# Three graph layers: from dense count and attention strips to sums over edge lists fetched by row

## What is computed

```python
# first layer: GCN with self loops, residual and layer norm
h = x @ W0;  norm = dinv[row] * dinv[col]
x1 = layernorm(x + segment_sum(h[row] * norm, col) + b0)
# then rgat_conv twice: 4 heads of 192 (then ELU), and 1 head of 768
xr = einsum('nd,rdf->rnf', x, W)
oi, oj = xr[etype, dst], xr[etype, src]
alpha = leaky_relu(oi @ q + oj @ k, 0.2)
e = exp(alpha - segment_max(alpha, dst)[dst])
out = segment_sum(e / segment_sum(e, dst)[dst] * oj, dst) + b
# result: layernorm(x1 + out2)
```

## Time and profile before

| | us |
|---|---|
| median of three runs | 1782.49 (1778.65 to 1787.3) |
| the profiled execution | 1783.22 |
| its span, first to last instruction | 1781.4 |
| mean granted TensorE clock | 0.941 of full |

### The profile page before, as it was taken

How to read it: one execution, slowest core, us unless ns; L and a number is a source line. 1 busy time by engine, 2 the same in 40 slices (tenths; PEclk the granted TensorE clock), 3 DMA queues, 4 the chain that set the end, 5 groups by cost and what they waited for, 6 DMA issues and landing times. The chain is left out here.

```text
span 1781.4 us, 27924 instructions
## 1 busy us (share of the span) xinstructions
PE 1589.1 (89%) x10121; PEld 1403.0 (79%) x10121; DVE 1240.1 (70%) x1980; ACT 580.8 (33%) x876; POOL 98.2 (6%) x58
## 2 busy tenths in 40 slices
PE   4999788978878799799979997959999989999996
PEld 4675354545548799799979997957999989999996
DVE  7346766656418999998999899943664275656774
ACT  2332122323312443354335434423222232224522
POOL 1000000000013001300310040000000000000000
PEclk8999899999988899999989998978999999999998
DMA  8674043245466655566366654426776646645652
GB/s 210 230 244 146 10 95 80 81 90 114 87 187 178 194 177 195 178 207 229 97 195 189 208 174 143 130 79 198 221 236 212 229 163 212 212 169 197 209 205 79
DMA packets 175693, 297.80 MB, mean 167 GB/s; under 512 B 35787, under 2 KB 118093, under 8 KB 175061
## 3 DMA queue, kind: packets, MB, share of 16 engines
q1 hardware_dynamic: 175476, 296.04, 54.3%
q10 hardware_dynamic: 96, 0.12, 0.0%
HBM read 227.41 MB, written 68.70 MB: 166 GB/s over the span
## 5 line engine op out<-in xcount | busy, mean ns | idle before, releaser
L1091 PE MATMUL ah_ps<-ah_xr,ah_T 125*125 125x194 f32 x2400 | 406.4, 333 | 41.2 <-issue 37.8
L1091 PEld LDWEIGHTS ah_ps<-ah_xr,ah_T 125*125 125x125 f32 x2400 | 403.0, 191 | 43.6 <-issue 38.6
L1666 PE MATMUL sl_ps<-sl_masks,sl_wH 125*125 125x256 f32 x1800 | 322.8, 282 | 10.6 <-DVE sl_wL L1506 9.6
L1666 PEld LDWEIGHTS sl_ps<-sl_masks,sl_wH 125*125 125x125 f32 x1800 | 275.6, 187 | 12.6 <-DVE sl_wL L1506 6.4
L923 ACT ACTIVATE ah_T<-ah_T,ah_kq 125x625 f32<-125x625 f32 x240 | 195.9, 817 | 223.6 <-DVE ah_T L1021 223.6
L1666 PE MATMUL sl_ps<-sl_masks,sl_wL 125*125 125x256 f32 x900 | 253.7, 282 | 0.0
L1004 DVE CUSTOM_DVE_ANT_0 ah_dump<-ah_krow,ah_gap 125x1250 bf16<-125x1250 f32 x120 | 206.1, 1781 | 14.5 <-DMA ah_krow<-ah_d_k 14.4
L1021 DVE SCALAR_TENSOR_TENSOR ah_T<-ah_rows,ah_k_rest 125x625 f32<-125x625 f32 x240 | 211.0, 881 | 0.4
L1028 DVE SCALAR_TENSOR_TENSOR ah_T<-ah_T,ah_cnt 125x625 f32<-125x625 f32 x240 | 192.4, 802 | 19.1 <-DMA ah_cnt<-d_C 17.4
L1666 PEld LDWEIGHTS sl_ps<-sl_masks,sl_wL 125*125 125x125 f32 x900 | 168.5, 187 | 0.0
L612 PE MATMUL fr_ps<-fr_col_hot,fr_row_hot 125*128 x516 | 119.0, 364 | 42.7 <-DVE fr_col_hot L406 38.1
(11 more groups left out here) (189 smaller groups left out, 2057.5 us busy)
## 6 DMA issues: line engine op xcount, KB each, us to landing
sl_masks<-sl_d_xr SPq DMA_DIRECT2D x60, 768.0 KB, 4.3
ah_gap<-d_gap SPq DMA_DIRECT2D x120, 312.5 KB, 3.6
ah_cnt<-d_C SPq DMA_DIRECT2D x240, 156.2 KB, 3.8
sl_d_xr<-sl_xs SPq DMA_DIRECT2D x60, 384.0 KB, 4.1
ah_rows<-ah_d_rows SPq DMA_DIRECT2D x24, 625.0 KB, 5.2
fr_raw<-in_w SPq DMA_DIRECT2D x36, 384.0 KB, 5.9
d_gap<-fr_gap SPq DMA_DIRECT2D x30, 312.5 KB, 2.5
d_C<-fr_C SPq DMA_DIRECT2D x15, 625.0 KB, 10.7
```

The lines of the kernel that those rows point to most:

```text
L1091: mm = pe.matmul(o, T[:, g % TR, t * P:(t + 1) * P], xr[:, r, j], start=(first and t % 2 == 0), stop=final, skip_group_check=True)
L1666: mm = pe.matmul(flat[:, u * TW:(u + 1) * TW], a[:, i % AR, ts], xr[:, i % LR, x, fs], start=(first and u % 2 == 0 and q == 0), stop=(last ...
```

## The change

Nearly the whole program is rewritten. The dense counts `d_C` and the strips go; all three layers sum over an edge list.

- `front` sorts nothing, but gives every edge a place so that each target tile starts at a pair of chunks: 88 pairs (NPAIR), 176 chunks (NCH) of 128 places, 22528 places for 20000 edges. A running count per tile (`tensor_tensor_scan`) and two small products give the places; 160 products of one-hots (`list_part`) write the lists `edge_src`, `edge_row`, `slot_dst`, `rel_hot`, `pair_tile`. Four chunks are a quad (44 of them), eight a piece (22).
- The gap table is filled with 1e30 by 30 stores and then marked by 160 scatters of 125 two-byte zeros (`mark`), each of which waits until the one before it has landed.
- In each layer `pair` multiplies one-hots of the targets (fp32) with 128 gathered source rows (fp32, 3 KB each), two chunks accumulating in PSUM, and `add_pair` adds the result to the tile's accumulator in SBUF at an index that is read at run time. The rows come from HBM by 176 indirect DMAs a layer from GpSimd's queue, in a ring of four quads that lies over xH and xL.
- `attention_heads` and `second_layer` become one function `relation_layer`, called with 4 heads (names `fl_`) and with 1 (`sl_`). Projections are 60 units of 384 columns in both and are sent to HBM as fp32 rows with a 1 and the source term k behind each head's columns. `pick` fetches every edge's target terms by products with one-hots; `alpha`, an exponential and `weighted_hot` put each edge's weight into its one-hot. The masked maximum stays. With 4 heads its gathers start after the last unit, and so do the picks; with 1 head the maxima and picks run beside the units. x and h stay in SBUF in split form between the stages.
- In the last layer products use fp32 instead of three float32r ones.

The core of the diff:

```diff
+            def mark(c):
+                if c:
+                    pool.wait_ge(gap_marked, 16 * c)
+                pool.indirect_dma_start(cells, bass.IndirectOffsetOnAxis(ap=gap_at[:, c:c + 1], axis=0), edge_gap[:], None)\
+                    .then_inc(gap_marked, 16)
+
+            for c in range(MARKS):
+                mark(c)
+            pool.wait_ge(h0_out, 32 * NT)
+            pool.wait_ge(rows_made, 1)
+            for i in range(2):
+                pool.wait_ge(s_out[i], 32 * UNITS // 2)
+            m = MARKS
+            for c in range(NCH):
+                if c >= 4 * QR and c % 2 == 0:
+                    pool.wait_ge(pair_done, (c - 4 * QR) // 2 + 1)
+                pool.indirect_dma_start(rows(c // 4)[:, c % 4], None, d_h0,
+                                        bass.IndirectOffsetOnAxis(ap=edge_src[:, c:c + 1], axis=0)).then_inc(gathered[c // 4 % QR], 16)
+                if c >= 4 and c % 5 in (0, 2, 4) and m < ET:
+                    mark(m)
+                    m += 1
...
+            pool.wait_ge(xr_done, NU)
+            for c in range(NCH):
+                if c >= 4 * QR and c % 2 == 0:
+                    pool.wait_ge(pair_done, (c - 4 * QR) // 2 + 1)
+                pool.indirect_dma_start(rows(c // 4)[:, c % 4], None, d_xr,
+                                        bass.IndirectOffsetOnAxis(ap=edge_row[:, c:c + 1], axis=0)).then_inc(gathered[c // 4 % QR], 16)
...
+            def add_pair(p, t):
+                v.wait_ge(pair_done, p + 1)
+                if p:
+                    v.wait_ge(added, p)
+                else:
+                    v.wait_ge(acc_zero, 1)
+                a = acc[:, bass.ds(t, 1)].rearrange("p o a d -> p (o a) d")
+                v.tensor_tensor(a, a, ps[0:P, 2 * (p % PR):2 * (p % PR) + 2, 0:SW], ALU.add).then_inc(added, 1)
...
+                for c in (2 * p, 2 * p + 1):
+                    r = rows(q)[:, c % 4]
+                    for a in range(2):
+                        o = ps[0:P, 2 * (p % PR) + a]
+                        if first:
+                            for s in range(HH):
+                                mm = pe.matmul(o[:, s * (W + 2):(s + 1) * (W + 2)], hot[:, q % 2, c % 4, a * HH + s],
+                                               r[:, a * SW + s * (W + 2):a * SW + (s + 1) * (W + 2)], start=(c % 2 == 0 and s == 0),
+                                               stop=(c % 2 == 1), skip_group_check=True)
+                        else:
+                            mm = pe.matmul(o[:, 0:SW], hot[:, q % 2, c % 4, 0], r[:, a * SW:(a + 1) * SW], start=(c % 2 == 0),
+                                           stop=(c % 2 == 1))
+                mm.then_inc(pair_done, 1)
```

More of the change, by code:

```diff
@@ L33 @@
 NO_EDGE = -1e30
-TG = 2
-NG = E // P // TG
-WIN = 25
-NW = N // WIN
-WCOLS = U * WIN
+ET = E // P
 PARTS = [(0, 112), (112, 13)]
 GROUPS = [(0, 500), (500, 500), (1000, 250)]
-HALF = N // 2
-HT = HALF // P
-ZC = FH + 2
+NPAIR = (E + NT * (2 * CH - 1)) // (2 * CH)
+NCH = 2 * NPAIR
+NQ = NCH // 4
+QR = 4
+PIECE = 8
+PW = PIECE * CH
+NPIECE = NCH // PIECE
+WHY = "a pair's tile is counted from the ends of nine tiles where the table is made"
 class Kit:
@@ L465, in _ @@
+            while m < ET:
+                mark(m)
+                m += 1
+            pool.wait_ge(gap_marked, 16 * ET)
         @block.scalar
@@ L1098, in second_layer @@
-def second_layer(kit, keep, d_h, wqk, d_gap, w, bias, residual, out, d_C):
+            pe.wait_ge(list_used, ET // LB)
+            pe.sem_inc(list_done, 1)
+            pe.wait_ge(h0_made, 2 * NT)
+            pe.wait_ge(dst_made, 1)
+            for a in range(2):
+                tr = pe.transpose(ps[0:NPAIR, 4, a * CH:(a + 1) * CH], slot_dst[:, a * NPAIR:(a + 1) * NPAIR], ident[:])
+            tr.then_inc(dst_turned, 1)
+            for p in range(NPAIR):
+                pair(p)
+            for t in range(NT):
+                turn_x1(t)
@@ L1184, in second_layer @@
[L1184 to L1190 removed]
+        dst_row_in = [S(f"dst_row_in{i}") for i in range(2)]
@@ new lines, in _ @@
+            v.wait_ge(added, NPAIR)
+            v.tensor_scalar(zr[:], acc_seg[:, :, K0:NSEG, W], Z_EPS, None, ALU.add).then_inc(zr_made, 1)
+            v.wait_ge(zr_made, 1)
+            link(v.reciprocal(zr[:], zr[:]))
+            if first:
+                for t in range(NT + 2):
+                    if t < NT:
+                        take(t)
+                    if 1 <= t <= NT:
+                        elu(t - 1)
+                    if t >= 2:
+                        low(t - 2)
+            else:
+                v.wait_ge(pre_made, NT)
+                for t in range(NT):
+                    take(t)
+                    variance(t)
+                    if t:
+                        scale_and_shift(t - 1)
+                scale_and_shift(NT - 1)
```

2025 lines of the change are left out of this document (844 added, 1181 removed).

## The result

The changed kernel takes **1960.96 us** (median of four runs, 1958.33 to 1964.48) against 1784.51 us for the kernel before in the same comparison (1778.65 to 1787.3). The ratio is 1.0995, with a 95% interval of 1.0959 to 1.103: the change costs 176 us. I had forecast 1820, 2% slower, so the sign was right and the size was not: 36 us of loss forecast, 176 measured. The profiled execution has a span of 1956.4 us.

A forecast was written before the change was run, and what follows sets the result against it. TensorE was taken to set the pace everywhere. Stages of 715 + 578 + 523 gave 1816 us of span, 1818 of execution, forecast as 1820 us; range 1650 to 2050, the forecast's own 1770 to 1915.

The forecast's parts named there:

- the products over edges: All three stages: 88 pairs of chunks take 239 us of TensorE in each.
- a projection stage: Heads' stage: weights, split products and 60 units take 211 us until the last unit; held the safest part.
- the masked maxima: Heads' stage: 120 maxima run beside the projections, end at 191 us and are hidden.
- the second layer: Last stage: projections 219, first gathers 6, loop 264, end 34, together 523 us where 590 stood.
- 0.6 us a quad: Second layer's loop: three engines within 0.7 us do not overlap fully, so 6.0 us a quad, 264 us in all.
- VectorE is the slowest engine: Heads' loop: VectorE needs 7.0 us a quad and hides TensorE's work; 44 quads take 308 us.
- rival 4: Loops: idle TensorE drops to its lower clock, at worst 84 us more in the first stage; no chance of its own.
- The chain is latest: First stage's gathers: chained marks at 3.7 us each set the pace, 385 us for 104, ending at 670 us.
- Ten tiles of variance, norm and split follow at 4 us: First stage's tail: ten tiles with the drain take 45 us, ending the stage at 715 us.
- Cheap marks: First stage: a mark costs 2.4 us, GpSimd's issue sets the pace, kernel 1711 to 1612 us, halfway 1660; chance 35%.
- The port conflict: Heads' loop and first stage: GpSimd and VectorE block each other, 97 and 48 us more, 1965 us together; chance 20%.
- Far slower marks: First stage: landing takes 5 us, a mark 6.2 us, 400 us more, kernel 2220 us; chance 5%.

## Why the prediction was right and wrong

**Right.** What the change removes was priced well: TensorE's sums go, the products over edges take 233 us at full clock where I said 239, a projection stage takes 217 us to its last unit in the heads (forecast 211), the masked maxima are hidden, the second layer is at 525 against 523. In that layer, though, two errors cancel, and that it comes within 2 us is luck: its first gather comes at 242 us instead of 225, since 22 pieces of picks, for which the sum had no term, stand among TensorE's units, 4.05 us from unit to unit there instead of 3.2, and its loop takes 250 us instead of 264. I had added 0.6 us a quad because three engines were close. They overlapped almost fully: through most of the loop TensorE's records follow one another without a gap, here for four quads.

```profile
1700.97 10.55 PE L1350 MATMUL sl_ps<-xL,sl_hot 128*125 128x386 f32 x32
1711.36 10.55 PE L1350 MATMUL sl_ps<-xH,sl_hot 128*125 128x386 f32 x32
```

(32 records are two quads, 5.2 us each.)

**Wrong: the heads' loop, 66 of the 77 us.** The step was "VectorE is the slowest engine ... 7.0 us; TensorE 5.4 plus 0.7 of picks hides below it". VectorE's price was high: its work was 6.35 us a quad. TensorE's was 6.8 in the changed kernel, at a clock of 0.86, and 6.1 as forecast once it was fed. The loop took 8.5, more than either. I added up each engine's work and took the larger, and never followed one quad round. The circle from weighted one-hots over pairs and the picks behind them in TensorE's order back to VectorE is longer than either engine's work. One line in TensorE's order made it, and moving that line gave back 76 us. The idle TensorE also ran at a clock of 0.86 there, which my rival 4 had put inside the ranges: two quads of products took it 12.75 us instead of 2 x 5.51, and since its work is a part of the circle, the slower clock made the circle longer. The other 11 us: the first weighted one-hots start 17 us later in the stage than forecast, and the stage's end is 6 us shorter.

**Wrong: the marks among the gathers, 43 of the 61 us.** The step was "The chain is latest: 104 x 3.7 = 385 us". It took 436 us, 4.19 a mark, and it was not the chain alone. (The gathers began at 271 us instead of 285, which hides some of the loss.) I compared 9.6 us of issue with 11.1 of chain for five gathers and three marks, again as if the larger of two hid the other. The issue is 5 x 1.26 + 3 x 1.52 = 10.9 us, with the 0.30 us between two DMAs, for which I had no row. The waits come on top of it and not beside it, because in an in-order queue a mark that is not yet allowed holds back the gathers behind it: 12.6 us. With two chains, where almost no mark waits, the same gathers and marks took 395 us instead of 440. The price of one mark by itself was well bounded: 3.76 us each ahead of the gathers, beside stores and loads, 2.9 alone. There the landing does count, 1.7 us of every 2.9. The page of the Trainium skill that I weighed, "DMA: Bandwidth & Descriptors", section "Anatomy of one DMA — SWDGE (gpsimd) path", has about 2.0 us for such a DMA; the traces have 2.9 for a mark with nothing beside it, and the measurement decides.

**Wrong: the first stage's tail, 18 of the 61 us.** 63 us from the last mark to the end instead of 45. The step was "Ten tiles of variance, norm and split follow at 4 us". A tile took 4.8 on average and 5.4 in the steady part, since norm, turn, copy and subtraction are in series; one tile of distance gave back 14 us. The pitch explains 8 of the 18 us; the rest lies before the first tile and after the last.

**The rivals.** (1) Cheap marks: out as a price; a mark would have had to cost under 3.4 us (the sum given for it comes to 3.48) and ran at 4.19. But its picture of the loop, GpSimd's issue as the pace, was nearer to what happened than the forecast's chain. (2) The port conflict: its sign and even its total (1965) fit the measured time, and it is still not the cause. Its own test was a gather over 1.75 us in the heads' loop with both engines waiting for it; the issues were 1.04 to 1.10 us on average, and the loop without gathers was no faster. In the first stage a mark's issue took 1.28 us on average, and 1.26 in the kernel with all marks ahead, not 0.3 more. A total that fits says nothing of the mechanism. The collision itself is real, 22 gathers at 1.92 us, and with the picks moved it decides which engine is full. (3) Far slower marks: out. (4) The lower clock was real (0.83 and 0.86 in the two starved loops, 0.99 and 0.94 once fed). In the first stage it was a companion of the waits, since GpSimd waited only 2.1 us for TensorE there; in the heads' loop it lengthened the circle, by an amount that no run isolates.

## What to carry to other kernels

In a loop over several engines, add up the work of each engine, and then also follow one item round through every wait, in each engine's own order. Where a consumer's small step stands in a producer's queue behind a big one that waits for the consumer, the two take turns, and the loop costs more than the work of either (8.5 us a quad here, for 6.35 and 6.8). When one such limit is gone, read the trace again: the next one may be an engine that looked harmless. A chain of DMAs in an in-order queue costs issue and gap of everything in it plus the landings that nothing covers; so count the instructions first, and ask of each whether its result is needed at all.

## What the runs showed of the hardware

- An indirect DMA costs GpSimd's queue 0.95 us for 128 rows of 3 KB and 1.19 to 1.22 us for 125 cells of two bytes, with 0.30 us before the next: the smaller transfer is the dearer issue here (one is a gather, the other a scatter; direction and size were not separated).
- A gather's issue that starts while VectorE runs a product of 2000 columns with both inputs in SBUF (2.24 us) takes 1.92 us on average in the changed kernel (22 of them) and 2.48 us with the picks moved (43), at most 2.99. Beside VectorE's additions of 776 columns, with one input in PSUM, it stays at 0.95 us (38 of them in the changed kernel).
- Chained two-byte scatters alone: one every 2.9 us (100 of them from 280.3 to 568.1 us) at a DMA share of 0.04; 1.7 us of that is the wait for the landing.
- Gathers of 3 KB rows run at 316 to 328 GB/s with the DMA engines at 0.93 to 0.95, level with TensorE's fp32 products. In one of three sets, each on its own chip, the same 176 gathers took 253 us, in loops that nothing but gathers held, instead of 227 to 236, while the kernel before took the same time in all three (1780.8, 1782.8, 1782.7 us).
- TensorE's granted clock followed how well it was fed: the same 704 records took 296.9 us at 0.83 and 233.5 at 0.99. A record in this loop took 486 ns in the median and 973 to 976 at most, the two levels, 2.4 and 1.2 GHz.
